# Two-layer graph kernel: the last products of a turn taken ahead of mixes and late jobs, late jobs of turns 2 to 4 spread over later units

## Chip, cores and metric

The kernel runs on 1 core of one Trainium2 chip. The metric is the device time of one execution in microseconds (us); lower is better.

## The reference, cut to what matters

```python
# x: [4096, 128], adj: [4096, 4096], float32
h = maximum(layernorm(x), 0)
msg = h @ W0 + B
sens = exp(-(1 / adj - 1) ** 2 / (2 * 0.5 ** 2))
x = x + where(adj < 1, sens, 0) @ msg                # layer 0
h = maximum(layernorm(x), 0)
A = adj + eye(4096)
d = sum(A, axis=1) ** -0.5
x = x + relu((d[:, None] * A * d[None, :]) @ (h @ W1.T))   # layer 1
```

Layer 1 needs `h` of all rows of the result of layer 0, so each tile of `adj` is used twice: once through the exponential for layer 0, and once as it is for layer 1.

## The kernel before

`adj` is cut into 8 x 8 blocks of 512 x 512. A **turn** g (0 to 7) is one block row, a **unit** u = 8g + idx one block; `ORDER` gives the block column of each unit, with the youngest columns of support last. Per unit these things are done:

- SP loads a pair of blocks as they lie in memory (`load`, L286 to L296, 16 transfers a pair, three pairs ahead). VectorE turns each block into `kept` (`turn`, L661), and masks it into `wt` (`cut`, L676). From turn 4 on it also sums the rows (`row_sum`, L669).
- ScalarE makes the weights in place: `log` (L542), `square` (L552, in turns 0 to 3 for half of the units or more by VectorE's `quad`, L682, instead), `invert` (L547) and `weigh` (L561 or L558). Its order in a unit is log(u), square(u-1) where it has it, invert(u), weigh(u-1).
- TensorE multiplies: `multiply_weights(u)` (L392, here **product u**) adds the block to `acc0`, two units later (`LAG` = 2). So the last two products of a turn stand in idx 0 and 1 of the next one. `sum_tiles(u)` (L423) sums rows in turns 0 to 3.
- Layer 1: where the support rows of a block's column are known already, `mix_once(u)` (L405, **mix u**) uses the block from `kept`. Where they aren't, the block goes to memory (`store`, L305) and is loaded back by POOL for a **late job** (r, c) (`mix_late`, L415), at the unit that the table `JOBS` names. Jobs not in the table come in `TAIL`, after the last unit. POOL loads them in the order of the table into three slots; a load waits until the job that had the slot before is done (L354).

At the end of a turn a chain runs over all engines, each step at the idx in `STEPS` (first value for turns before 5, second later): ScalarE's `copy_x1t` (L587) at idx 1 or 2 waits for the turn's last product; TensorE's `turn_sums` (L430, idx 1) gives VectorE the row sums of turns 0 to 3 (`own_rows`, L744, idx 2), which wait at the head of VectorE's queue; TensorE's `turn_x1` (L446, idx 2 or 3); VectorE's `make_x1` (L758 to L776, idx 3 or 4), whose end is `hid`; TensorE's `turn_hid` (L452, idx 4 or 5, taken ahead of the unit's other work); ScalarE's `log_pows` and `copy_hid` (L591, L599, at the end of idx 3 or 4); TensorE's `multiply_support` (L458, idx 5 or 6, ahead too); VectorE's `make_support` (L686 to L787, idx 5 or 7). Each engine takes its instructions in program order, and waits at semaphores, so a step that comes late holds up all that stands behind it on its engine.

Five `wt` buffers and four `kept` buffers tie the engines: `cut(u)` waits for product u-5, `turn(u)` for the store and the mix of unit u-4.

The order of TensorE's work within a unit is written out by hand in the loop at L469 to L495.

Of the kernel before, what the change touches and what calls it, by code (L numbers as in the profile page):

```python
# [24 lines left out]
LAG = 2  # L25
# [10 lines left out]
def col(u):  # L36

    return ORDER[u // G][u % G]


def at_once(u):

    return col(u) < u // G
# [12 lines left out]
def once_count(u):  # L56
# [2 lines left out]

JOBS = {15: [(0, 0)], 22: [(0, 1)], 23: [(1, 1)],
# [5 lines left out]
        (2, 7), (3, 7), (4, 7), (5, 7), (6, 7), (7, 7), (0, 7), (1, 7)]  # L68
IN_TURN = [job for u in sorted(JOBS) for job in JOBS[u]]
LOADED = IN_TURN + [job for job in TAIL if job != (G - 1, G - 1)]  # L70
# [4 lines left out]
PE_SUMS = 4  # L75
# [14 lines left out]
def step_at(g, idx, name):  # L90

    return g >= 1 and idx == STEPS[name][g >= EARLY_TURNS]
# [10 lines left out]
def first_job(u):  # L103

    return sum(len(JOBS[v]) for v in JOBS if v < u)

# [19 lines left out]
def build(nc, x, adj, w0, b0, w1, out):  # L126
# [6 lines left out]
    with ctx:  # L133
# [230 lines left out]
        def _(pe):  # L364
            def turn_h0(c):
                pe.wait_ge(h0_done, c + 1)
                if c >= 1:
                    pe.wait_ge(h0_t_done, c)
                for a in range(8):
                    last = nc.tensor.transpose(turn_bank[a // 4][:, (a % 4) * P:(a % 4 + 1) * P],  # L370
                                               support[:, c * 8 + a, :], ident[:])
                last.then_inc(h0_turned, 1)

            def multiply_msg(c):
                pe.wait_ge(h0_t_done, c + 1)
                if c >= 1:
                    pe.wait_ge(msg_done, c)
                for a in range(8):
                    src = (hid_t, x1t)[a // 4]
                    last = nc.tensor.matmul(msg_bank[a // 4][:, (a % 4) * P:(a % 4 + 1) * P],  # L380
                                            src[:, (a % 4) * P:(a % 4 + 1) * P], w0_sb[:], start=True, stop=True)
                last.then_inc(m_multiplied, 1)

            def multiply_weights(u):
                first, last = u % G == 0, u % G == G - 1
                pe.wait_ge(wt_done, u + 1)
                if u < G and u % 2 == 0:
                    pe.wait_ge(msg_done, u // 2 + 1)
                if first and u >= G:
                    pe.wait_ge(x1t_copied, u // G)  # L390
                for k in range(T):
                    mm = nc.tensor.matmul(acc0[:], msg[:, col(u) * T + k, :], wt[:, u % WTS, k, :],  # L392
                                          start=(first and k == 0), stop=(last and k == T - 1))
                mm.then_inc(acc0_done, 1)

            def mix_once(u):
                g, c = u // G, col(u)
                pe.wait_ge(turned, u + 1)
                if c == g - 1:
                    pe.wait_ge(sup_done, g)  # L400
                first = [v for v in range(g * G, g * G + G) if at_once(v)][0] == u
                if first and g >= 6:
                    pe.wait_ge(evicted, g - 5)
                for k in range(T):
                    mm = nc.tensor.matmul(once_bank[g][:], support[:, c * T + k, :], kept[:, u % KEPT, k, :],  # L405
                                          start=(first and k == 0), stop=False)
                mm.then_inc(once_done, 1)

            def mix_late(j, bank, start, stop):
                r, c = LOADED[j]  # L410
                slot = late_slot(j)
                pe.wait_ge(late_loaded[slot], 16 * slot_count(j))
                pe.wait_ge(sup_done, c + 1)
                for k in range(T):
                    mm = nc.tensor.matmul(bank[:], support[:, c * T + k, :], late_tile(slot)[:, k, :],  # L415
                                          start=(start and k == 0), stop=(stop and k == T - 1))
                mm.then_inc(late_done, 1)

            def sum_tiles(u):
                pe.wait_ge(turned, u + 1)  # L420
                bank = sum_bank[u // G]
                for k in range(T):
                    mm = nc.tensor.matmul(bank[k * B:(k + 1) * B, :], ones[:], kept[:, u % KEPT, k, :],  # L423
                                          start=(u % G == 0), stop=(u % G == G - 1))
                mm.then_inc(tiles_summed, 1)

            def turn_sums(g):
                pe.wait_ge(sums_copied, g + 1)
                for a in range(T):
                    mm = nc.tensor.matmul(side[:, a:a + 1], hid_t[:, a * P:(a + 1) * P], thirty_second[:],  # L430
                                          start=True, stop=True)
                mm.then_inc(quads_summed, 1)

            def sum_quads(g):
                pe.wait_ge(summed, C4 * (g + 1 - PE_SUMS))
                if g == PE_SUMS:
                    pe.wait_ge(quads_done, 2)
                nc.tensor.matmul(side[:, 0:T * Q * C4], quad_sum[:].rearrange("p q i -> p (q i)"),
                                 rowpart[:, g % 2].rearrange("p a q c -> p (a q c)"),
                                 start=True, stop=True).then_inc(quads_summed, 1)  # L440

            def turn_x1(g):
                pe.wait_ge(x1t_copied, g + 1)
                pe.wait_ge(rows_owned, g + 1)
                for a in range(T):
                    last = nc.tensor.transpose(side[:, a * P:(a + 1) * P], x1t[:, a * P:(a + 1) * P], ident[:])  # L446
                last.then_inc(x1_turned, 1)

            def turn_hid(g):
                pe.wait_ge(hid_done, g + 1)  # L450
                for a in range(T):
                    last = nc.tensor.transpose(side[:, a * P:(a + 1) * P], hid[:, a, :], ident[:])  # L452
                last.then_inc(hid_turned, 1)

            def multiply_support(g):
                pe.wait_ge(hid_t_done, g + 1)
                for a in range(T):
                    mm = nc.tensor.matmul(side[:, a * P:(a + 1) * P], hid_t[:, a * P:(a + 1) * P], w1t[:],  # L458
                                          start=True, stop=True)
                mm.then_inc(sup_multiplied, 1)  # L460
# [8 lines left out]
            for u in range(UNITS):  # L469
                g, idx = u // G, u % G  # L470
                if g == 0 and idx % 2 == 0:
                    turn_h0(idx // 2)
                    multiply_msg(idx // 2)
                if g > PE_SUMS and step_at(g, idx, "sum_quads"):
                    sum_quads(g - 1)
                if step_at(g, idx, "turn_hid"):
                    turn_hid(g - 1)
                if step_at(g, idx, "multiply_support"):
                    multiply_support(g - 1)
                if g < PE_SUMS:  # L480
                    sum_tiles(u)
                if at_once(u) and idx < G - 1 and not (g >= 6 and idx == 0):
                    mix_once(u)
                if 1 <= g <= PE_SUMS and step_at(g, idx, "sum_quads"):
                    turn_sums(g - 1)
                if step_at(g, idx, "turn_x1"):
                    turn_x1(g - 1)
                if u >= LAG:
                    multiply_weights(u - LAG)
                for i, (r, c) in enumerate(JOBS.get(u, [])):  # L490
                    mix_late(first_job(u) + i, mix[r], r == 0 and c == 0, (r, c) in ((0, 4), (1, 5)))
                if g >= 6 and idx == 0:
                    mix_once(u)
                if g >= 1 and idx == G - 1:
                    mix_once(u)  # L495
# [376 lines left out]
```

## Time and profile before

| | |
|---|---|
| median of 3 runs | 612.91 us (612.34 to 613.88) |
| profiled execution | 612.8 us, of which span 611.0 us |
| busy: TensorE matmul | 536.8 us (88%) |
| busy: VectorE | 472.7 us (77%) |
| busy: ScalarE | 462.2 us (76%) |
| busy: GpSimd (POOL) | 41.4 us (7%) |
| mean granted TensorE clock | 0.975 of full speed |
| memory traffic | 145.19 MB, mean 238 GB/s |

Busy shares are means over the whole span. The span is the time from the first to the last instruction of the profiled execution; the execution's time is 1.8 us more. Records of matmuls overlap by some tenths of a microsecond, so a group of eight shown as 3.60 in the timeline is 3.43 in the chain, which cuts overlaps.

### The profile page before, as it was taken

To read this page: it belongs to the slowest core of one execution; us is meant where nothing else is said; L and a number is where in the kernel's file an instruction comes from. 1 tells how busy PE (TensorE), PEld (TensorE's weight loads), DVE (VectorE), ACT (ScalarE), POOL (GpSimd) and SP (SyncE) were. 2 spreads that over 40 slices of the span, in tenths; PEclk is the share of its full clock that TensorE was granted. 3 is DMA by queue.
4 is the path that set the end of the run, shared out by engine and by line. 5 is a ranking of instruction groups with operands and counts; after the bars stand their busy time and mean duration, and the time that the engine had idled before them with its cause. 6 is when DMAs were issued, how large, how long until landed. Compare 5 with 4: busy or idle time off the path is not lost.

```text
span 611.0 us, 4974 instructions
## 1 busy us (share of the span) xinstructions
PE 536.8 (88%) x1579; PEld 240.1 (39%) x1579; DVE 472.7 (77%) x552; ACT 462.2 (76%) x305; POOL 41.4 (7%) x68
## 2 busy tenths in 40 slices
PE   2468878889799987898699997899999999999994
PEld 1244423333244432344344443344444444445442
DVE  5899879998999378988999859993899959202156
ACT  2398999998999379966999987998499976910010
POOL 0344200000000000000000000000000000111000
PEclk9998998899999999899899999899999999999998
DMA  6989999999999987978969959789497401299222
GB/s 171 224 257 336 326 337 343 331 357 367 354 340 268 264 205 221 277 214 284 300 150 273 198 201 289 209 218 264 159 255 212 104 28 70 76 419 393 74 65 73
DMA packets 93340, 145.19 MB, mean 238 GB/s; under 512 B 10369, under 2 KB 84354, under 8 KB 84354
## 3 DMA queue, kind: packets, MB, share of 16 engines
q1 hardware_dynamic: 88274, 108.17, 63.8%
q0 software_dynamic: 5040, 36.70, 16.6%
q8 instruction: 12, 0.20, 0.1%
q14 instruction: 14, 0.11, 0.1%
HBM read 106.04 MB, written 38.80 MB: 237 GB/s over the span
## 4 chain that ended last, share of the span: by engine, by line
PE 51%; ACT 32%; DVE 11%; issue 3%; SPq 2%; DMA 1%; DVEq 0%
PE acc L392 18%; PE mix L405 14%; PE mix L415 13%; ACT wt L542 8%; ACT wt L547 8%; ACT wt L561 7%; ACT wt L552 6%; DVE kept L661 3%; DVE wt L676 3%; ACT wt L558 2%; PE acc L415 2%; PE mix L423 1%; PE side L415 1%; SPq L294 1%; DVE bn L697 1%
## 5 line engine op out<-in xcount | busy, mean ns | idle before, releaser
L392 PE MATMUL acc<-wt,msg 128*128 128x512 f32 x512 | 243.8, 621 | 30.8 <-ACT wt L561 26.8
L392 PEld LDWEIGHTS acc<-wt,msg 128*128 128x128 f32 x512 | 97.2, 197 | 162.8 <-issue 115.9
L661 DVE STREAM_TRANSPOSE kept<-raw 128x2048 f32<-128x2048 f32 x64 | 147.5, 2305 | 6.0 <-DMA adj_t_spill<-kept 4.4
L676 DVE SCALAR_TENSOR_TENSOR wt<-kept 128x2048 f32<-128x2048 f32 x64 | 146.5, 2289 | 2.3 <-PE acc L392 0.7
L542 ACT ACTIVATE wt<-wt 128x2048 f32<-128x2048 f32 x64 | 121.7, 1902 | 13.6 <-DVE wt L676 13.6
L547 ACT ACTIVATE wt<-wt 128x2048 f32<-128x2048 f32 x64 | 121.7, 1901 | 0.5
L405 PE MATMUL mix<-kept,support 128*128 128x512 f32 x224 | 100.9, 595 | 1.0 <-ACT mixed L603 1.0
L415 PE MATMUL mix<-late,support 128*128 128x512 f32 x208 | 95.1, 601 | 2.5 <-DVE support L787 2.5
L561 ACT ACTIVATE wt<-wt 128x2048 f32<-128x2048 f32 x50 | 95.0, 1901 | 0.0
L552 ACT ACTIVATE wt<-wt 128x2048 f32<-128x2048 f32 x50 | 94.9, 1899 | 0.0
L669 DVE TENSOR_REDUCE rowpart<-raw 128x16 f32<-128x4096 f32 x16 | 70.1, 4381 | 0.0
L405 PEld LDWEIGHTS mix<-kept,support 128*128 128x128 f32 x224 | 41.8, 190 | 53.5 <-issue 53.5
L415 PEld LDWEIGHTS mix<-late,support 128*128 128x128 f32 x208 | 39.9, 193 | 52.6 <-issue 52.6
L360 POOL DMA_DIRECT2D late<-adj_t_spill x26 | 13.9, 536 | 473.5 <-PE mix L415 398.0
L423 PE MATMUL mix<-kept,ones 128*32 128x512 f32 x256 | 36.5, 644 | 6.8 <-DVE kept L661 6.7
L758 DVE TENSOR_TENSOR x<-side,x 128x512 f32<-128x512 f32 x8 | 5.5, 689 | 46.7 <-PE side L446 46.7
L682 DVE SCALAR_TENSOR_TENSOR wt<-wt 128x2048 f32<-128x2048 f32 x14 | 32.0, 2289 | 12.0 <-ACT wt L547 11.9
L587 ACT COPY x1t<-acc 128x512 f32<-128x512 f32 x8 | 4.7, 582 | 39.8 <-PE acc L392 39.8
L558 ACT ACTIVATE wt<-wt 128x2048 f32<-128x2048 f32 x14 | 26.5, 1895 | 0.0
L645 ACT COPY kept<-mix 128x512 f32<-128x512 f32 x6 | 3.5, 585 | 29.9 <-PE mix L415 26.6
L599 ACT COPY hid_t<-side 128x512 f32<-128x512 f32 x8 | 4.6, 574 | 27.1 <-PE side L452 27.1
L345 POOL TENSOR_SCALAR support<-x,mv 128x128 f32<-128x128 f32 x24 | 21.9, 928 | 40.1 <-DVE mv L701 40.1
(87 smaller groups left out, 251.5 us busy)
## 6 DMA issues: line engine op xcount, KB each, us to landing
raw<-in_adj_dram SPq DMA_DIRECT2D x512, 128.0 KB, 4.8
adj_t_spill<-kept SPq DMA_DIRECT2D x35, 1024.0 KB, 9.0
late<-adj_t_spill POOLq DMA_DIRECT2D x26, 1024.0 KB, 7.2
raw<-adj_t_spill POOLq DMA_DIRECT2D x9, 1024.0 KB, 9.0
x<-in_x_dram SPq DMA_DIRECT2D x32, 64.0 KB, 2.5
out_dram<-kept SPq DMA_DIRECT2D x32, 64.0 KB, 1.8
w_sb<-in_L_gnn_W_dram SPq DMA_DIRECT2D x1, 64.0 KB
late<-in_L_gnn_W_dram SPq DMA_DIRECT2D x1, 64.0 KB
```

Of the source, the lines that this page charges most:

```text
L392: mm = nc.tensor.matmul(acc0[:], msg[:, col(u) * T + k, :], wt[:, u % WTS, k, :], start=(first and k == 0), stop=(last and k == T - 1))
L405: mm = nc.tensor.matmul(once_bank[g][:], support[:, c * T + k, :], kept[:, u % KEPT, k, :], start=(first and k == 0), stop=False)
L415: mm = nc.tensor.matmul(bank[:], support[:, c * T + k, :], late_tile(slot)[:, k, :], start=(start and k == 0), stop=(stop and k == T - 1))
L423: mm = nc.tensor.matmul(bank[k * B:(k + 1) * B, :], ones[:], kept[:, u % KEPT, k, :], start=(u % G == 0), stop=(u % G == G - 1))
L542: nc.scalar.activation(v, v, ACT.Ln, bias=LN_GUARD).then_inc(ln_done, 1)
L547: nc.scalar.activation(v, v, ACT.Exp, scale=-1.0).then_inc(inv_done, 1)
L552: nc.scalar.activation(v, v, ACT.Square, bias=-1.0).then_inc(square_done, 1)
L558: nc.scalar.activation(v, v, ACT.Exp, scale=-2.0, bias=-2.0).then_inc(wt_done, 1)
L561: nc.scalar.activation(v, v, ACT.Exp, scale=-2.0).then_inc(wt_done, 1)
L661: nc.vector.transpose(dst, src).then_inc(turned, 1)
L669: nc.vector.tensor_reduce(dst, src, AX_X, ALU.add).then_inc(summed, 1)
L676: nc.vector.scalar_tensor_tensor(out=wt[:, u % WTS], in0=v, scalar=CUTOFF, in1=v, op0=ALU.is_lt, op1=ALU.mult).then_inc(cut_done, 1)
```

## The change

TensorE's program alone is touched, and the table of late jobs. In idx 0 and 1 of every turn from 1 on, the product of two units before is taken ahead of `turn_sums` and `mix_once`. Five late jobs of turns 2 to 4 go to later units: (0,1) from 22 to 26, (1,1) from 23 to 28, (0,2) from 30 to 31, (1,2) from 31 to 34, (2,2) from 33 to 35. As POOL's loads wait for freed slots, they move with the jobs.

```diff
-JOBS = {15: [(0, 0)], 22: [(0, 1)], 23: [(1, 1)],
-        30: [(0, 2)], 31: [(1, 2)], 33: [(2, 2)],
+JOBS = {15: [(0, 0)], 26: [(0, 1)], 28: [(1, 1)],
+        31: [(0, 2)], 34: [(1, 2)], 35: [(2, 2)],
         38: [(0, 3)], 39: [(1, 3)], 41: [(2, 3)], 43: [(3, 3)],
...
                 if g < PE_SUMS:
                     sum_tiles(u)
+                if g >= 1 and idx < LAG:
+                    multiply_weights(u - LAG)
+                if 1 <= g <= PE_SUMS and step_at(g, idx, "sum_quads"):
+                    turn_sums(g - 1)
                 if at_once(u) and idx < G - 1 and not (g >= 6 and idx == 0):
                     mix_once(u)
-                if 1 <= g <= PE_SUMS and step_at(g, idx, "sum_quads"):
-                    turn_sums(g - 1)
                 if step_at(g, idx, "turn_x1"):
                     turn_x1(g - 1)
-                if u >= LAG:
+                if idx >= LAG:
                     multiply_weights(u - LAG)
```

## Rows read from the trace of the kernel before

**Rows 1.** The page: chain that ended last, shares by engine.

```profile
PE 51%; ACT 32%; DVE 11%; issue 3%; SPq 2%; DMA 1%; DVEq 0%
```

**Rows 2.** Windows: us; busy of PE, PEld, DVE, ACT, POOL; clock; DMA share; GB/s.

```profile
93.90:185.00 91.10, 80.90 (x276) 32.11 (x275) 86.02 (x84) 88.11 (x56) 1.04 (x2) 0.95 1.07 348
204.00:320.00 116.00, 101.70 (x300) 43.80 (x298) 96.89 (x86) 91.75 (x60) 1.58 (x3) 0.97 0.87 238
...
217.40:250.90 33.50, 26.55 (x96) 10.63 (x92) 28.53 (x35) 33.41 (x22) 0.00 (x0) 0.95 0.94 248
...
281.00:320.00 39.00, 31.65 (x81) 14.07 (x79) 38.65 (x38) 39.00 (x26) 0.53 (x1) 0.96 0.80 235
320.00:562.00 242.00, 232.75 (x579) 105.60 (x580) 175.50 (x156) 190.34 (x120) 13.14 (x25) 0.99 0.70 209
```

**Rows 3.** Timeline, ScalarE: start us, us, line, tiles; before copies of turns 0-3.

```profile
96.31 0.59 ACT L587 COPY x1t<-acc 128x512 f32<-128x512 f32 x1 [0.70 <-PE acc L392]
151.22 0.59 ACT L587 COPY x1t<-acc 128x512 f32<-128x512 f32 x1 [1.84 <-PE acc L392]
217.37 0.59 ACT L587 COPY x1t<-acc 128x512 f32<-128x512 f32 x1 [13.36 <-PE acc L392]
280.85 0.59 ACT L587 COPY x1t<-acc 128x512 f32<-128x512 f32 x1 [10.76 <-PE acc L392]
```

**Rows 4.** Chain that ended last in order of time, 185 to 225 us.

```profile
193.45 3.43 PE mix L415 x8
...
208.38 0.99 PE mix L423 x8
209.37 3.63 PE mix L405 x8
213.00 0.79 PE side L430 x8
213.79 3.56 PE acc L392 x8
```

**Rows 5.** Timeline, ScalarE: the weights of unit 23.

```profile
196.23 1.90 ACT L558 ACTIVATE wt<-wt 128x2048 f32<-128x2048 f32 x1
```

**Rows 6.** Timeline, turn 3: turned hid, support, VectorE and ScalarE.

```profile
228.90 0.60 PE L452 MATMUL side<-ident,hid 128*128 128x128 f32 x4
...
232.41 0.19 ACT L591 ACTIVATE inv<-pows 128x8 f32<-128x8 f32 x1
...
236.09 1.05 PE L458 MATMUL side<-w1t,hid_t 128*128 128x128 f32 x8
...
239.41 2.30 DVE L661 STREAM_TRANSPOSE kept<-raw 128x2048 f32<-128x2048 f32 x1
...
248.70 2.29 DVE L676 SCALAR_TENSOR_TENSOR wt<-kept 128x2048 f32<-128x2048 f32 x1
...
251.38 1.89 ACT L542 ACTIVATE wt<-wt 128x2048 f32<-128x2048 f32 x1
```

**Rows 7.** Timeline, turn 4: turned hid, ScalarE after it, product 35.

```profile
295.54 0.60 PE L452 MATMUL side<-ident,hid 128*128 128x128 f32 x4
...
297.54 0.20 ACT L591 ACTIVATE inv<-pows 128x8 f32<-128x8 f32 x1
...
305.57 3.70 PE L392 MATMUL acc<-wt,msg 128*128 128x512 f32 x8 [3.29 <-ACT wt L561]
```

**Rows 8.** Timeline, TensorE: products 28 and 44, each after a wait.

```profile
245.97 5.28 PE L392 MATMUL acc<-wt,msg 128*128 128x512 f32 x8 [2.50 <-ACT wt L561]
...
377.88 5.40 PE L392 MATMUL acc<-wt,msg 128*128 128x512 f32 x8 [4.15 <-ACT wt L561]
```

**Rows 9.** Windows: a burst of transfers in turn 3, columns as in rows 2.

```profile
217.00:228.00 11.00, 9.25 (x35) 3.42 (x35) 9.13 (x18) 10.60 (x7) 0.00 (x0) 1.00 1.07 258
```

**Rows 10.** Waits of VectorE, 93.9 to 185 us: total, times, longest.

```profile
DVE wt L682 <- ACT wt L547: 3.5, 3, 1.8
```

**Rows 11.** The page: DMA issues of late tiles.

```profile
late<-adj_t_spill POOLq DMA_DIRECT2D x26, 1024.0 KB, 7.2
```

## Prediction

> **What bounds the kernel now.** I read four views in this order. The chain that ended last gives TensorE half of the span and ScalarE a third [rows 1], so one share names no single bound; the stretches must be read. By stretches [rows 2]: from 320 us on TensorE is busy for 232.75 of 242.00 us. There TensorE's own work sets the time. Between 217.4 and 250.9 it is busy 26.55 of 33.50 us while ScalarE is full (33.41), and between 281 and 320 busy 31.65 of 39.00 us with ScalarE full (39.00). In these two stretches ScalarE leads and TensorE has 6.95 and 7.35 us to spare. The timeline says where ScalarE loses time: before its copies of acc0 to x1t for turns 0 to 3 it sits idle 0.70, 1.84, 13.36 and 10.76 us, each time until L392 is done [rows 3]. So twice TensorE is full while ScalarE waits, and then ScalarE is full while TensorE waits. That is an order fault, not a lack of engine: the copy needs the last product of a turn, and other TensorE work stands ahead of it. After the copy of turn 3 comes the PE-bound rest, which starts earlier by whatever the alternation no longer costs.
>
> **Prices of the moved pieces** [rows 4]: one late job is 3.43 us (8 records), one mix at an accumulation's start 3.63, the turned sums (L430) 0.79, one tile sum (L423) 0.99, one product 3.43 to 3.63. Nothing is added or removed; SP's transfers keep their order, and POOL's too, though POOL's wait for a free slot moves with the jobs.
>
> **End of turn 0 (units 8, 9).** Only L430 goes behind the product. ScalarE waits 0.70 us for it; I book nothing, bounds 0 and 0.7.
>
> **End of turn 1.** Same edit; L430's 0.79 us plus a gap of 0.1 comes off a wait of 1.84 [rows 3, 4]. ScalarE leads turn 2, so it is kept: **0.9 us**.
>
> **End of turn 2 (units 22 to 25).** Late jobs (0,1) and (1,1) leave (2 x 3.43 = 6.86) and mix 25 and L430 go behind product 23 (3.63 + 0.79 = 4.42): 11.3 us. Mix 24 changes places with product 22, which moves nothing for product 23. The copy starts at 217.4 - 11.3 = 206.1, ScalarE's wait shrinks from 13.36 to 2.1. The product must find its weights: those of unit 23 are ready at 198.1 [rows 5], product 23 would start at 202.5, so no new wait stands at the head of TensorE's queue.
>
> Now what is late next. From 206.1 TensorE does L430 0.79, mix 25 3.63, sum 0.99, turned x1 0.43, product 24 3.6, late (0,1) 3.43, sum 0.99, product 25 3.63 and the turned hid 0.5: it ends at 224.1. ScalarE comes to its copy of hid at 232.4 - 11.3 = 221.1 [rows 6] and waits 3.0; the gain is down to 8.3. In the kernel before TensorE was 2.9 us early there. Late (1,1) then delays multiply_support: 224.1 + 0.99 + 3.6 + 3.43 + 1.05 = 233.2, against 237.1; VectorE, which waits for it in make_support, keeps only some 5.1 us (it can start its scaling at 233.2 and its next turn at 234.3, against 239.4). VectorE's cut of unit 31 was done 0.4 us before ScalarE's log [rows 6], so ScalarE's gain falls to 5.1 + 0.4 = 5.5 and it would reach the next copy at 270.1 - 5.5 = 264.6.
>
> **End of turn 3 (units 31 to 33).** TensorE from 233.2: sum, product 27, sum, product 28 to 242.4; then sum 31 needs VectorE's turn 31, at 243.6; sum 0.99, product 29, late (0,2), mix 31, product 30, mix 32, product 31 = 6 pieces of about 3.5: 265.5. Late jobs (1,2) and (2,2), mix 33 and L430 are out of the way. Copy at 265.5 instead of 280.85: a gain of 15.3, with ScalarE waiting 0.9. The weights of unit 31 are ready three ScalarE passes of 1.9 us ahead of 264.6, by 258.9; its product starts at 261.9.
>
> After it: L430, mix 33, turned x1, product 32, late (1,2), product 33, late (2,2), turned hid: 265.5 + 0.79 + 3.63 + 0.5 + 3.6 + 3.43 + 3.6 + 3.43 + 0.5 = 284.9. ScalarE arrives at 297.5 - 15.3 = 282.2 [rows 7] and waits 2.7. Gain left: **12.7 us**. Product 35 started at 305.57 after a wait of 3.29 for its weights [rows 7]; it now starts at 292.9 after a wait of similar length. Both engines are 12.7 earlier, and from product 37 on TensorE hardly pauses, so the rest shifts as a block.
>
> **Turns 5 to 7.** Jobs stay. Moving mixes behind the products frees ScalarE earlier for its copies of turns 4 to 6, but each is followed by the turned hid, whose place in TensorE's work doesn't change. TensorE leads there [rows 2]: booked at nothing, bound a gain of 1 (its pauses there come to 9 us in all, mostly elsewhere).
>
> **Sum:** 0.9 + 12.7 = 13.6 us off. A second route agrees. TensorE's pauses from 217.4 to product 35 are 6.95 and 7.2 us, and two products in there take about 5.3 instead of 3.6 (3.4 us, one of them in [rows 8]): 17.6. What I leave is 1.2 before sum 31 and 3.4 before product 35: 4.6, so 13.0 plus the 0.9 = 13.9. The profiled execution took 612.8 us (span 611.0), the median of the three runs is 612.9. 612.8 - 13.6 = **599.2 us**.
>
> **The clock.** After waits of 2.50 and 4.15 us a product took 5.28 and 5.40 us (eight records), after 3.29 us another took 3.70 [rows 7, 8]; the granted clock of the two stretches with waits is 0.95 and 0.96, that of the long rest 0.99 [rows 2], so in them the clock was for some microseconds at 1.2 instead of 2.4 GHz. The slow product at 377.88 lies in TensorE's own stretch; if it or its like vanishes, 1.8 us each more come off; a new one at the now pause of 3.4 us would cost 1.6. The Trainium skill, "TensorE: Matmul & The Clock Gate", Part 1, says that the clock is halved when TensorE has idled, and comes back only after it has been busy again. By it the product after the 3.4 us pause would start slow and the sum would be about 12.0, or 600.8 us.
>
> **Rivals.**
> - **Transfers set the pace.** 204 to 320 us moves 238 GB/s x 116 us = 27.6 MB [rows 2]; in 13 us less that is 268 GB/s, while a burst in turn 3 with the engines' share at 1.07 moved only 258 [rows 9]. Were 258 the ceiling, the stretch would take 107 us, 9 off: 604; were it the 248 of turn 3's mean, 111 us, 4.7 off: 608. Against it: 93.9 to 185 sustained 348 GB/s at share 1.07 [rows 2], and VectorE's longest sum of waits in it is 3.5 us, for ScalarE; for transfers it is less [rows 10]. A row load is asked for three pairs ahead. The Trainium skill, "DMA: Bandwidth & Descriptors", Specifications, gives a core about 358 GB/s of HBM; by this rule no transfer binds and the sum stands.
> - **The copy's wait isn't TensorE's order.** If product 23 stood at the head of the queue for something else, the two mixes behind it would wait with it and nothing would be won: 612.8. The full TensorE in that stretch and weights ready at 198.1 [rows 5] speak against it.
> - **Slower: the late jobs block the turned hid.** The moved jobs stand ahead of turned hid or multiply_support in turns 3 and 4, where the kernel before had slack 2.9 and 1.4 us [rows 6, 7]. If ScalarE can't use the earlier copy, (0,1) delays it 0.5, (1,2) with (2,2) about 1.6 (6.86 less pauses near 3.9 and slack 1.4), and VectorE's make_support is late by some 2: 4 us more, 617. It decides once the gains at the two copies fall below the waits of 3.0 + 2.7 us. It needs gains well under half of the waits there are to win [rows 3]. A late tile that landed late would do it too, but they land in 7.2 us [rows 11] and are asked for by 232, used from 274.
>
> **Chances.** Forecast 0.78 (its own range 594.5 to 602.5: two slow products less, and each of the two copy waits misjudged by 1.5), transfers 0.13, no effect 0.05, slower 0.04. The likeliest is 599.2. The range of 594.5 to 606 takes in the transfer case at 604 and leaves out its worst part, and the last two. A measurement of this kernel tells about 0.3% from no change: faster 0.91, same 0.05, slower 0.04.
>
> **What would show it.** Right: waits before the copies of turns 2 and 3 of about 2 and 1 us, the copies near 205 and 265; new waits of about 3 us before the copies of hid in both turns; product 35 near 292; late jobs in TensorE's former pauses; from 320 us on the same picture, 13 to 14 us earlier. Wrong: VectorE's turns waiting for raw tiles (transfers), waits of TensorE for weights before products 22, 23, 30 or 31 (order), waits before the copies of hid above 5 us (the slower case), or TensorE pausing longer after 307.

## The result and the profile after

The changed kernel takes 598.92 us, median of 4 runs (597.56 to 599.75), against 613.25 us of the kernel before beside it: ratio 0.9765 (0.9743 to 0.9788), 14.3 us less. The profiled execution took 598.8 us, its span is 597.0. Forecast were 599.2 us in a range of 594.5 to 606. In the kernel after, lines behind the edit are numbered up to two higher (L587 is L589, L599 is L601).

The page of the kernel after, the chain that ended last, shares by engine [rows 1]:

```profile
PE 57%; ACT 15%; SPq 13%; DVE 10%; issue 4%; DMA 2%; DVEq 0%
```

ScalarE's share of the chain fell from 32% to 15%, and TensorE's grew from 51% to 57%. SP's issuing (SPq) rose from 2% to 13%: in the first turns, which the edit hardly touches, the chain here leads back through SP's loads. Part of this is chance. A second trace of the unchanged kernel has 50% TensorE, 24% ScalarE and 8% SPq, so the shares alone don't show what the edit did; the windows and waits below do.

Windows of the kernel after, columns as in [rows 2]; the first is turn 3 between the copy of x1t and tile sum 31, the second turn 4 from that copy to product 37, the third the rest to the tail:

```profile
206.20:243.20 37.00, 36.00 (x127) 14.97 (x126) 30.61 (x38) 33.02 (x22) 1.06 (x2) 1.00 1.02 299
...
265.40:307.80 42.40, 38.75 (x104) 18.22 (x104) 42.05 (x40) 39.95 (x26) 1.05 (x2) 0.96 1.03 296
307.80:548.00 240.20, 232.25 (x580) 105.37 (x579) 176.96 (x157) 189.75 (x120) 13.15 (x25) 0.99 0.71 212
```

In turn 3 TensorE pauses 1.0 us of 37.0, where it paused 6.95 of 33.50 before; in turn 4 3.65 of 42.4, against 7.35 of 39.00. The fullest engine of turn 4 is now VectorE, with 42.05 of 42.40 us (38.65 of 39.00 before). The long rest holds 232.25 us of TensorE work, against 232.75: it moved as a block.

Timeline of the kernel after, ScalarE's copies of x1t for turns 1, 2 and 3 [rows 3]:

```profile
152.18 0.59 ACT L589 COPY x1t<-acc 128x512 f32<-128x512 f32 x1 [1.43 <-PE acc L392]
...
206.19 0.59 ACT L589 COPY x1t<-acc 128x512 f32<-128x512 f32 x1 [1.28 <-PE acc L392]
...
265.37 0.59 ACT L589 COPY x1t<-acc 128x512 f32<-128x512 f32 x1 [1.12 <-PE acc L392]
```

The waits of 13.36 and 10.76 us before the copies of turns 2 and 3 are 1.28 and 1.12, and these copies come 11.2 and 15.5 us earlier. Then what is late next, timeline of turn 3 of the kernel after [rows 6]:

```profile
223.40 0.60 PE L452 MATMUL side<-ident,hid 128*128 128x128 f32 x4
...
224.03 0.59 ACT L601 COPY hid_t<-side 128x512 f32<-128x512 f32 x1 [2.60 <-PE side L452]
...
243.19 2.29 DVE L678 SCALAR_TENSOR_TENSOR wt<-kept 128x2048 f32<-128x2048 f32 x1
...
243.21 1.07 PE L423 MATMUL mix<-kept,ones 128*32 128x512 f32 x8 [1.01 <-DVE kept L663]
...
245.51 1.91 ACT L544 ACTIVATE wt<-wt 128x2048 f32<-128x2048 f32 x1 [1.10 <-DVE wt L678]
```

ScalarE waits 2.60 us for the turned hid, TensorE 1.01 us for VectorE's turn 31, and ScalarE's log of unit 31 waits 1.10 for its cut, 5.9 us earlier than in [rows 6]. In turn 4 [rows 7]:

```profile
284.31 0.59 ACT L601 COPY hid_t<-side 128x512 f32<-128x512 f32 x1 [1.18 <-PE side L452]
...
292.25 5.40 PE L392 MATMUL acc<-wt,msg 128*128 128x512 f32 x8 [3.65 <-ACT wt L563]
```

ScalarE waits 1.18 us for the turned hid, and product 35 comes at 292.25, 13.3 us earlier, after a pause of 3.65. It takes 5.40 us instead of 3.70; such a product is called slow here.

Waits of VectorE in the kernel after from 200 to 320 us, the whole answer:

```profile
DVE support L789 <- PE side L458: 5.9, 1, 5.9
DVE wt L684 <- ACT wt L549: 2.9, 2, 1.8
```

No transfer is among them, with 299 and 296 GB/s in the two windows above, more than in the burst of [rows 9]. The 5.9 us are VectorE's wait for multiply_support in turn 3, by which the prediction let its gain fall from 11.3 to 5.1 us. What the prediction didn't book is another wait that went: before, VectorE stood idle for TensorE's row sums (L430) in the same stretch, by its waits:

```profile
DVE pows L744 <- PE side L430: 12.2, 2, 7.5
```

### The profile page after: what moved, and what is told of

Its sections match the earlier page's. It is cut to its first block, busy times and chain, and to the rows that moved or that the text cites. A ratio compares the mean times of both kernels' runs of the same rounds, so it can differ in the third digit from the quotient of the medians.

```text
span 597.0 us, 4974 instructions
## 1 busy us (share of the span) xinstructions
PE 533.6 (89%) x1579; PEld 239.9 (40%) x1579; DVE 472.3 (79%) x552; ACT 463.0 (78%) x305; POOL 41.4 (7%) x68
## 4 chain that ended last, share of the span: by engine, by line
PE 57%; ACT 15%; SPq 13%; DVE 10%; issue 4%; DMA 2%; DVEq 0%
PE acc L392 21%; PE mix L405 14%; PE mix L415 14%; SPq L294 10%; ACT wt L549 4%; ACT wt L544 4%; DVE kept L663 3%; ACT wt L563 3%; ACT wt L554 3%; DVE wt L678 3%; SPq L301 2%; DMA adj_t_spill<-kept 2%; PE acc L415 2%; PE mix L423 2%; PE side L415 1%
## 5 line engine op out<-in xcount | busy, mean ns | idle before, releaser
L415 PE MATMUL mix<-late,support 128*128 128x512 f32 x208 | 93.4, 592 | 1.2 <-DVE support L789 1.2
L601 ACT COPY hid_t<-side 128x512 f32<-128x512 f32 x8 | 4.7, 582 | 31.2 <-PE side L452 31.2
L828 DVE TENSOR_TENSOR kept<-mix,support 128x512 f32<-128x512 f32 x6 | 4.1, 690 | 19.2 <-PE mix L506 19.2
```

## Experiments

Each was timed on one chip together with the kernel before, whose median there is named. Executions of one kernel lie within 2 to 7 us of each other, so a median of six is good to about 0.3%. The traces give a sharper measure: the time from ScalarE's copy of x1t of turn 1 (all that is before it varies by up to 2.7 us with the stores, below) to that of turn 7. Starts of the copies, from the timelines, in us:

| kernel | turn 1 | turn 2 | turn 3 | turn 7 | 1 to 7 |
|---|---|---|---|---|---|
| before | 151.22 | 217.37 | 280.85 | 546.35 | 395.1 |
| before, again | 152.70 | 217.85 | 279.75 | 545.29 | 392.6 |
| after | 152.18 | 206.19 | 265.37 | 532.40 | 380.2 |
| after, again | 153.17 | 207.21 | 266.39 | 533.37 | 380.2 |
| order only | 151.40 | 212.22 | 271.24 | 536.59 | 385.2 |
| order only, again | 151.66 | 213.49 | 272.78 | 539.40 | 387.7 |
| jobs only | 151.40 | 209.74 | 270.09 | 535.44 | 384.0 |
| jobs only, again | 152.85 | 211.21 | 271.56 | 536.92 | 384.1 |
| late turns in old order | 150.50 | 205.45 | 264.63 | 531.66 | 381.2 |
| two jobs ahead of hid | 152.54 | 207.50 | 269.50 | 537.16 | 384.6 |
| spread | 152.86 | 207.81 | 265.65 | 531.00 | 378.1 |
| spread, again | 151.96 | 205.97 | 263.81 | 530.86 | 378.9 |
| spread, turn 5 too | 152.46 | 206.48 | 264.32 | 528.54 | 376.1 |
| the same, (0,4) later | 153.09 | 208.04 | 265.88 | 527.72 | 374.6 |

Single slow instructions move these stretches too. Product 18, in turn 2, starts after the same wait of 2.07 us in all fourteen traces. It takes 3.70 us in eight of them and 5.40 in six: before, order only again, late turns in old order, two jobs ahead of hid, spread (the first), and (0,4) later. Where it is slow the way from turn 1 to turn 2 is 0.9 to 1.0 us longer (54.95 against 54.01 us with the new order and jobs). So where two kernels do the same up to turn 2, the time from turn 2 to turn 7 compares them better.

**Each part alone.** Order only is the changed kernel with

```diff
-JOBS = {15: [(0, 0)], 26: [(0, 1)], 28: [(1, 1)],
-        31: [(0, 2)], 34: [(1, 2)], 35: [(2, 2)],
+JOBS = {15: [(0, 0)], 22: [(0, 1)], 23: [(1, 1)],
+        30: [(0, 2)], 31: [(1, 2)], 33: [(2, 2)],
```

> Edit: the new order in idx 0 and 1, with the late jobs at their old units. Theory (both parts fill the same TensorE pauses of turns 3 and 4): the copy of x1t of turn 2 comes 4.4 us earlier (mix 25 and L430 out of its way), near 213; no late job stands ahead of the turned hid of turn 3, so ScalarE keeps the 4.4; the copy of turn 3 comes 4.4 earlier again, near 272. Together 8.8 us off, about 604.4. Rival 1 (the order is all, the moved jobs only shift work): 599 as with the whole change. Rival 2 (the parts add up without sharing): the job part would then be worth 14.3 less 8.8.

Measured: 605.4 us (before 611.59), ratio 0.9892 (0.9863 to 0.9921). Timeline, ScalarE's copy of x1t of turn 2, of hid in turn 3, of x1t of turn 3:

```profile
212.22 0.59 ACT L589 COPY x1t<-acc 128x512 f32<-128x512 f32 x1 [8.09 <-PE acc L392]
...
227.37 0.56 ACT L601 COPY hid_t<-side 128x512 f32<-128x512 f32 x1
...
271.24 0.59 ACT L589 COPY x1t<-acc 128x512 f32<-128x512 f32 x1 [6.29 <-PE acc L392]
```

The places are the expected ones (213 and 272), and the copy of hid has no wait. This run also answers a question that the prediction leaves aside: whether the late row sums, which VectorE waits for, set the pace instead of ScalarE's copy of x1t. With the order alone the row sums of turn 2 (L430) start 60.6 us after the copy of turn 1, as in the second trace of before, and VectorE waits 6.55 us for them, as there. Yet the copy of x1t comes 4.3 us earlier by the same comparison, and so does the copy of hid behind it. So it is ScalarE's copy that counted.

Jobs only is the kernel before with

```diff
-JOBS = {15: [(0, 0)], 22: [(0, 1)], 23: [(1, 1)],
-        30: [(0, 2)], 31: [(1, 2)], 33: [(2, 2)],
+JOBS = {15: [(0, 0)], 26: [(0, 1)], 28: [(1, 1)],
+        31: [(0, 2)], 34: [(1, 2)], 35: [(2, 2)],
```

> Edit: the late jobs at their new units, with the old order in idx 0 and 1. Theory: the copy of x1t of turn 2 comes 6.9 us earlier, near 210.5, and ScalarE meets the turned hid of turn 3 with a wait near 0; the copy of turn 3 has mix 33 and L430 still ahead of product 31 and comes near 270, 10.9 earlier; 10.9 off, about 602.3. The two parts alone come to some 19.7 us, against 14.3 together, as both fill the same pauses. Rival (parts add up): 14.3 less what the order alone gives. Rival (late jobs only block the turned hid, no gain of their own): 613 or slower.

Measured: 603.97 us (before 611.59), ratio 0.9873 (0.984 to 0.9907). Timeline, ScalarE's copies of x1t of turns 2 and 3:

```profile
209.74 0.59 ACT L587 COPY x1t<-acc 128x512 f32<-128x512 f32 x1 [5.62 <-PE acc L392]
...
270.09 0.59 ACT L587 COPY x1t<-acc 128x512 f32<-128x512 f32 x1 [5.45 <-PE acc L392]
```

Again both are within a microsecond of what was expected, so each part wins by its own mechanism; neither only shifts idle time. But the medians are 2.6 and 3.3 us short of the expectations, and the gains of 6.2 and 7.6 add up to the whole 14 rather than to 19.7. So all three were run again beside each other.

> The changed kernel once more, beside its two parts on one chip. If the parts draw on the same pauses, it is clearly less than the sum of them: in the traces product 37 came 12.2 us earlier with both, 8.1 with the order alone and 9.2 with the jobs alone (17.3 together). If they add up, it is their sum. Expected: 14 off, ratio 0.977.

> The order alone once more. Shared pauses: 8 us off by the trace's product 37, ratio 0.987. Adding up: 6.5 off, ratio 0.9893, as the first timing gave.

> The jobs alone once more. Shared pauses: 9 us off by the trace's product 37, ratio 0.985. Adding up: 7.5 off, ratio 0.9877.

Measured, with the kernel before at 612.36 us: whole change 599.81, ratio 0.9798 (0.9767 to 0.9828); order 605.52, 0.989 (0.9863 to 0.9916); jobs 604.55, 0.9882 (0.9851 to 0.9914). That is 12.6 off, against 6.8 and 7.8. In time the parts add up to 14.6; that is 2.1 us over the whole, inside the error of these medians (0.3% is 1.8 us for each).

**The kernel before, traced again.**

> The kernel before, unchanged, to see which of the profiled execution's lines are chance. From the copy of x1t of turn 1 to that of turn 7 it took 395.1 us in the first trace, and 380.2 in two traces of the changed kernel. Theory (shared pauses, as predicted): again 395. Rival (the first trace of before had a slow product more than usual, 5.32 us at 385.81): 393.4, and the parts alone then give 6.9 and 9.3 by the same stretch, as timed (6.5 and 7.7). Time the same as before within 0.3%.

Measured: 613.5 us (the other runs of it there 613.66), ratio 1.0006 (0.998 to 1.0031), and a stretch of 392.6 us from turn 1 to 7, not 395.1. But the reason given for it was wrong: the late job (0,4) was slow again (5.37 us). What it lacks are the slow products 18 and 28 of the first trace. Timeline of TensorE, product 28, to be held against [rows 8]:

```profile
246.46 3.70 PE L392 MATMUL acc<-wt,msg 128*128 128x512 f32 x8 [2.50 <-ACT wt L561]
```

The same wait of 2.50 us, and 3.70 instead of 5.28 us. By the mean of both traces of before (393.9) the stretch is shorter by 7.4 with the order (mean of two), 9.8 with the jobs and 13.7 with both. So the traces show some sharing (17.2 against 13.7). The times can't tell: the first set has 13.8 for the parts against 14.3, the second 14.6 against 12.6. How far the parts overlap stays open, between nothing and some 3.5 us.

**The order in turns 5 to 7.**

```diff
-                if g >= 1 and idx < LAG:
+                if 1 <= g < 5 and idx < LAG:
                     multiply_weights(u - LAG)
...
-                if idx >= LAG:
+                if idx >= LAG or g >= 5:
                     multiply_weights(u - LAG)
```

> Edit: the changed kernel, with the old order in idx 0 and 1 of turns 5 to 7. Theory: the order there is worth nothing, as TensorE leads: 598.9 within 0.6. Rival: the 1.7 us that came off between products 44 and 45 of turn 5 come from the new order there, and not from chance of the clock: 600.6.

Measured: 598.12 us (before 611.59), ratio 0.9777 (0.9748 to 0.9805). The order there is worth nothing that shows. From turn 2 to turn 7 this kernel takes 326.21 us, the changed one 326.21 and 326.16; the 1.0 us more in the table is the slow product 18. Timeline of TensorE at product 44 and the late job (0,4) of this kernel:

```profile
364.85 6.71 PE L392 MATMUL acc<-wt,msg 128*128 128x512 f32 x8 [4.15 <-ACT wt L563]
372.77 3.67 PE L415 MATMUL mix<-late,support 128*128 128x512 f32 x8 [1.21 <-DVE support L789]
```

The job takes 3.67 us after 1.21, as in the kernel after, though the order is the old one.

**Two late jobs ahead of the turned hid.**

```diff
-JOBS = {15: [(0, 0)], 26: [(0, 1)], 28: [(1, 1)],
+JOBS = {15: [(0, 0)], 26: [(0, 1)], 27: [(1, 1)],
```

> Edit: the changed kernel with late job (1,1) at unit 27 instead of 28, so that two late jobs stand ahead of the turned hid of turn 3. Theory (a job ahead of the turned hid is paid by ScalarE): its wait before the copy of hid of turn 3 grows from 2.60 to 6.0 us; multiply_support keeps its place; the weights of unit 29 come about 2 us later, product 29 with them, and the copy of turn 3 too, near 267.5; 2 us slower than the changed kernel. Rival (VectorE's and TensorE's own work hide it): the same as the changed kernel.

Measured: 602.0 us (before 612.36, whole change 599.81), ratio 0.9841 (0.9809 to 0.9873). Timeline, ScalarE's copy of hid in turn 3 and TensorE's product 28:

```profile
228.77 0.59 ACT L601 COPY hid_t<-side 128x512 f32<-128x512 f32 x1 [6.03 <-PE side L452]
...
242.27 5.40 PE L392 MATMUL acc<-wt,msg 128*128 128x512 f32 x8 [2.39 <-ACT wt L563]
```

The wait is 6.03 us, as worked out. The median is 2.2 us more than that of the whole change, but the intervals touch (0.9809 to 0.9873 and 0.9767 to 0.9828), so the size is uncertain. The copy of turn 3 comes 62.0 us after that of turn 2, against 59.2. The loss enters one product earlier than expected: product 28 waits 2.39 us for its weights and is slow, and 1.7 of the 2.8 us are that slowness. This is the mechanism of the slower rival, at a size that the two copies' gains of 11 to 15 us easily carry.

**Spread further.**

```diff
-JOBS = {15: [(0, 0)], 26: [(0, 1)], 28: [(1, 1)],
-        31: [(0, 2)], 34: [(1, 2)], 35: [(2, 2)],
+JOBS = {15: [(0, 0)], 28: [(0, 1)], 29: [(1, 1)],
+        31: [(0, 2)], 34: [(1, 2)], 36: [(2, 2)],
```

> Edit: the changed kernel, with late job (0,1) at unit 28 instead of 26, (1,1) at 29 instead of 28, (2,2) at 36 instead of 35, so that no late job of turn 3 and one less of turn 4 stands ahead of the turned hid. Theory: ScalarE's waits for the turned hid (2.60 and 1.18 us in the changed kernel) go, TensorE's pause of 1.0 before tile sum 31 goes, and that of 3.65 before product 35 shrinks by about 2 with no slow product after it: 3 us less than the changed kernel, about 596. Rival (TensorE's work bounds turns 3 and 4 and the waits are hidden): 598.9. Rival (the jobs now delay products 26 to 36 instead): 600 or more.

> The spread version once more, beside the two above. Theory: 2 us less than the changed kernel, ratio 0.975. Rival (the first timing was chance): ratio 0.977 to 0.980, as the changed kernel.

Measured: 596.61 us (before 611.59), ratio 0.975 (0.9722 to 0.9778), and 596.31 (before 613.66), ratio 0.973 (0.9696 to 0.9765). The stretch from turn 1 to 7 is 1.3 to 2.1 us shorter than with the change. Timeline, ScalarE's copy of hid in turn 3; TensorE's product 34 and mix 38:

```profile
222.96 0.56 ACT L601 COPY hid_t<-side 128x512 f32<-128x512 f32 x1
...
282.85 3.70 PE L392 MATMUL acc<-wt,msg 128*128 128x512 f32 x8 [1.73 <-ACT wt L563]
...
295.86 3.70 PE L405 MATMUL mix<-kept,support 128*128 128x512 f32 x8 [1.44 <-DVE kept L663]
```

The waits before both copies of hid and the pause before product 35 are gone; in their place stand 1.73 us before product 34 and 1.44 before mix 38, which waits for VectorE's turn. From turn 2 to turn 7 the first trace takes 323.2 us, against 326.2 in both traces of the changed kernel: the 3 us expected. The second takes 324.9, with late job (0,4) slow (5.37 us). By time alone the difference to the changed kernel isn't settled.

Then the same rule in turn 5:

```diff
-        38: [(0, 3)], 39: [(1, 3)], 41: [(2, 3)], 43: [(3, 3)],
+        38: [(0, 3)], 39: [(1, 3)], 44: [(2, 3)], 45: [(3, 3)],
```

> Edit: the spread version of before this one, with late jobs (2,3) at unit 44 instead of 41 and (3,3) at 45 instead of 43. Theory (the same rule applied to turn 5: a late job ahead of the turned x1 delays VectorE, ScalarE and so product 44, which TensorE waits 4.15 us for): turned x1 and hid come 3.4 us earlier, the pause of 4.15 before product 44 shrinks to 0.7, with no slow product after it; 3.4 to 5 us less than the spread version, 592 to 593. Rival (TensorE's work is all that counts from unit 37 on): the same as the spread version, 596.5.

Measured: 594.65 us (before 613.66, spread version 596.31), ratio 0.9705 (0.9672 to 0.9739): only 1.7 less than the spread version, short of the 3.4 to 5 expected. Timeline, ScalarE's copy of hid in turn 5; TensorE's product 44 and late job (0,4):

```profile
351.59 0.59 ACT L601 COPY hid_t<-side 128x512 f32<-128x512 f32 x1 [2.15 <-PE side L452]
...
360.03 3.70 PE L392 MATMUL acc<-wt,msg 128*128 128x512 f32 x8 [0.71 <-ACT wt L563]
367.96 5.37 PE L415 MATMUL mix<-late,support 128*128 128x512 f32 x8 [4.23 <-DVE support L789]
```

The pause before product 44 fell from 4.15 to 0.71 us as expected, but 4.23 us stand now before the late job, which waits for VectorE's make_support of turn 5 and is slow. So the pause has moved to the next wait, and the job was moved too:

```diff
-        46: [(0, 4)], 47: [(1, 4)], 49: [(2, 4)], 51: [(3, 4)], 53: [(4, 4)],
+        47: [(0, 4), (1, 4)], 49: [(2, 4)], 51: [(3, 4)], 53: [(4, 4)],
```

> Edit: the version with turn 5 spread, with late job (0,4) taken in unit 47 ahead of (1,4), behind product 45, instead of in unit 46. In the version with turn 5 spread TensorE paused 0.71 us before product 44 but then 4.23 us before late job (0,4), for VectorE's make_support, and that job was slow (5.37 us). Theory (the pause moved to the next wait): product 45 finds its weights at 367.2 and starts 6 us earlier, the pause there is 3.5 us; with (0,4) behind it the following mix starts 2.5 us earlier: 592.2. Rival (the pause only moves again, or product 45 is the slow one): 594.6, the same.

Measured: 593.01 us (before 613.58), ratio 0.9675 (0.9644 to 0.9706), 20.6 us less than the kernel before. Timeline of TensorE, products 44 and 45 and both late jobs:

```profile
361.60 3.70 PE L392 MATMUL acc<-wt,msg 128*128 128x512 f32 x8 [0.72 <-ACT wt L563]
368.80 3.70 PE L392 MATMUL acc<-wt,msg 128*128 128x512 f32 x8 [3.50 <-ACT wt L563]
372.34 7.03 PE L415 MATMUL mix<-late,support 128*128 128x512 f32 x16
```

Product 45 starts after 3.50 us and isn't slow, and the jobs follow without a wait. The stretch from turn 1 to turn 7 is 1.5 us shorter than in the version before and 5.6 shorter than in the changed kernel, though product 18 is slow here. From turn 2 to turn 7 it is 319.7 us against 322.1, 2.4 less, which is what was expected.

## Why the prediction was right, step by step

- **What bounds it.** Right. TensorE and ScalarE took turns in waiting for each other in turns 3 and 4, and TensorE led from there on. The block from product 37 on kept its work (232.25 against 232.75 us).
- **End of turn 1, 0.9 us.** Not seen. The copy came at 152.18 instead of 151.22. The wait before it did shrink, from 1.84 to 1.43 us, but ScalarE was late by itself. Timelines of VectorE show why, its turn of units 8 and 10, each waiting for a store, first of the kernel before:

```profile
78.69 2.31 DVE L661 STREAM_TRANSPOSE kept<-raw 128x2048 f32<-128x2048 f32 x1 [2.91 <-DMA adj_t_spill<-kept]
...
91.56 2.31 DVE L661 STREAM_TRANSPOSE kept<-raw 128x2048 f32<-128x2048 f32 x1 [1.48 <-DMA adj_t_spill<-kept]
```

  and of the kernel after:

```profile
79.15 2.31 DVE L663 STREAM_TRANSPOSE kept<-raw 128x2048 f32<-128x2048 f32 x1 [3.20 <-DMA adj_t_spill<-kept]
...
92.93 2.31 DVE L663 STREAM_TRANSPOSE kept<-raw 128x2048 f32<-128x2048 f32 x1 [2.39 <-DMA adj_t_spill<-kept]
```

  The first of them, with 3.20 us instead of 2.91, stands before any instruction that was changed. Over all fourteen traces these waits are 1.0 to 4.2 and 1.0 to 2.9 us, so a term of 0.9 us can't be told from chance in the place of the copy: it comes at 150.50 to 153.17 us in the ten traces with the new order (152.2 on the mean), at 151.22 to 152.85 in the four without (152.0). The wait before it is shorter with the new order, 1.6 us on the mean against 2.3, which agrees with the term; but ScalarE then arrives later by as much. Whether that is chance or follows from the edit stays open, and no run here shows the 0.9 in the time.
- **End of turn 2.** Right in size, lucky in the place: 206.1 was worked out without the 0.9 of turn 1, with it 205.2; measured were 206.19. From the copy of turn 1 it is 54.0 us, 0.9 fewer than worked out, as product 18 wasn't slow this time. The first trace of before has a slow product 18 in there; the second, without it, has 65.15 us, and 65.15 less 54.01 is 11.1 for the 11.3 forecast. That VectorE's wait for the row sums goes with the late jobs isn't in the prediction, and changed nothing in its sum.
- **What is late next in turn 3.** Right: waits of 3.0 and 1.2 us worked out, 2.60 and 1.01 measured; tile sum 31 at 243.6, measured 243.21.
- **End of turn 3.** Right: 265.5, measured 265.37, with a wait of 1.12 for 0.9. But the gain is measured from a trace with product 28 slow. From the copy of turn 2 to that of turn 3 the changed kernel takes 59.2 us, the first trace of before 63.5, the second 61.9. So of the 4.3 us won here only 2.7 are won against an execution without that slow product.
- **After it.** The turned hid was to hold ScalarE 2.7 us; it was 1.18, since VectorE's cut had already held ScalarE for 0.76. Product 35 was worked out at 292.9, with the 0.9 of turn 1 at 292.0; it came at 292.25. Its pause of 3.4 was 3.65 and it was slow.
- **The clock.** The branch put at 1.6 us came true: the product after that pause took 5.40 us (granted clock of that stretch 0.96, so for some of it 1.2 GHz), and product 37 is 12.2 us earlier, not 13.6. The branch on the other side came true too. Timeline of TensorE, late job (0,4) of the kernel before:

```profile
385.81 5.32 PE L415 MATMUL mix<-late,support 128*128 128x512 f32 x8 [2.53 <-DVE support L787]
```

  and product 44 and the same job in the kernel after:

```profile
365.59 6.68 PE L392 MATMUL acc<-wt,msg 128*128 128x512 f32 x8 [4.15 <-ACT wt L563]
373.52 3.67 PE L415 MATMUL mix<-late,support 128*128 128x512 f32 x8 [1.25 <-DVE support L789]
```

  The pair ends 1.7 us sooner, as the job is no longer slow. The two branches cancel: that the sum of 13.6 stands so close to 14.3, though its 0.9 wasn't seen, is partly luck. By the Trainium skill, "TensorE: Matmul & The Clock Gate", Part 1, the clock is halved when TensorE has idled. The slow product 35 after 3.65 us agrees with that, but no length of wait decides it here: with two jobs ahead of hid the same product took 3.70 us after 3.66, while product 18 of before took 5.40 after 2.07.
- **Turns 5 to 7, nothing.** Right, tried by itself (326.21 us from turn 2 to turn 7 with either order).
- **The rivals.** Transfers: refuted, 299 GB/s and no wait of VectorE for one. The Trainium skill, "DMA: Bandwidth & Descriptors", Specifications, puts the limit of a core at HBM at about 358 GB/s. These windows stay below it, but it is no ceiling of this kernel: from 522 to 537 us the changed kernel moved 427 GB/s. Order of no effect: refuted by 6.2 and 6.8 us for the order alone. Slower: its mechanism is real (6.03 us of wait with one job more ahead of hid), its size too small.
- **What the experiments' expectations had too large** is the parts alone (8.8 and 10.9, timed 6.2 to 7.8). Both were taken from the first trace of before, with products 18 and 28 slow. With the jobs alone neither was slow, so their 1.0 and 1.6 us were counted as won: from turn 1 to turn 3 that kernel takes 118.7 us, 10.9 less than the first trace of before and 8.4 less than the second. With the order alone product 28 was slow again (5.14 and 5.40 us), so the traces show the 4.4 us of turn 3 against the first trace and less against the second. That every median falls short isn't fully explained.

## What to carry to other kernels

When two engines wait for each other in turn, look for the one instruction that the next stage needs and take it ahead of work that nobody waits for; then place the displaced work behind the next hand-over, not in front of it, and check each following wait, since the pause moves there. Work out such a change along the queue of each engine with the times of one trace: here the starts worked out from the end of turn 2 on, without the 0.9 of turn 1, came within 0.7 us, while a slow matmul or a late store moves the whole by 1 to 2 us in any single trace. Before you credit an edit with a slow instruction that has vanished, trace the old kernel twice.

## What was not expected of the hardware

The same wait at the same place does not give the same clock. By the traces:

| instruction | wait before it, us | took, us |
|---|---|---|
| product 18, all kernels | 2.07 | 3.70 in eight traces, 5.40 in six |
| product 28, before and order only | 2.50 | 3.70 in one, 5.14 to 5.40 in three |
| product 35, before and order only | 3.29 | 3.70 in three, 6.77 in one |
| product 35, with the new jobs | 3.65 | 5.33 to 5.40 in five, 3.70 in one |
| product 44, all but the last two kernels | 4.15 | 5.26 to 6.71 in twelve |

The late job (0,4) behind product 44 took 5.30 to 5.37 us in four of those twelve traces and 3.67 in eight, and nothing in the program tells them apart: the change of its order in turns 5 to 7 doesn't (3.67 with either), and the first traces of order only and of before have the same 5.40 us for product 44, with 3.67 and 5.32 behind it.
